# A feed-forward inside an attention stage changes its two PSUM banks and its place in every engine's order; a second one gets a second pair of activation buffers

## The reference

```
x += attention_a0(norm(x))   # 16 heads of 16, softmax
x += ffn0(norm(x))           # one 256x256 product with a bias
x += attention_b0(norm(x))   # 4 heads of 64, softmax, biases
x += ffn0(norm(x))           # the same weights again
x += retention_1(norm(x))    # 16 heads, decaying mask, no softmax
x += ffn1(norm(x))           # 256 -> 1024 gated, Hadamard, -> 256
x += attention_b1(norm(x))   # per token, over heads
x += ffn1(norm(x))
```

## Time and profile before

| | |
|---|---|
| median of 3 runs | 1296.91 us (1292.14 to 1298.73) |
| the profiled execution's own time | 1294.7 us |
| its span in the trace | 1292.9 us |
| PE busy | 1053.2 us, 81% |
| DVE busy | 696.3 us, 54% |
| ACT busy | 389.5 us, 30% |
| POOL busy | 321.3 us, 25% |
| mean granted clock of TensorE | 0.84 |

### The profile page before, as it was taken

One profiled execution on the slowest core, in us unless ns is written; L12 is line 12 of the kernel. 1 busy time (PEld: TensorE's weight loads), 2 busy tenths in 40 slices (PEclk: granted clock), 3 DMA queues, 4 the chain that ended last, 5 costly groups with the idle time before them and its releaser, 6 DMA issues.

```text
span 1292.9 us, 21462 instructions
## 1 busy us (share of the span) xinstructions
PE 1053.2 (81%) x8114; PEld 930.1 (72%) x8114; DVE 696.3 (54%) x1410; ACT 389.5 (30%) x711; POOL 321.3 (25%) x356
## 2 busy tenths in 40 slices
PE   3589878757887874688878999998888897789998
PEld 3466655456776764565656999997788887689998
DVE  4478765535455445587765554545455555534443
ACT  1146544412333220233324332322122221222332
POOL 5300100125633663312101021110033333332000
PEclk9679997859999996787777999986677775599999
DMA  8734320000010000174530000235656556210000
GB/s 237 223 117 145 118 86 3 1 1 17 18 66 17 1 1 0 58 209 135 142 113 1 1 1 1 56 76 98 122 112 120 109 111 118 37 33 10 17 18 17
DMA packets 147431, 89.39 MB, mean 69 GB/s; under 512 B 109632, under 2 KB 136256, under 8 KB 146560
## 3 DMA queue, kind: packets, MB, share of 16 engines
q1 hardware_dynamic: 142960, 70.45, 23.0%
q10 hardware_dynamic: 2944, 12.59, 3.4%
q0 software_dynamic: 1424, 4.98, 1.3%
HBM read 54.16 MB, written 33.55 MB: 68 GB/s over the span
## 4 chain that ended last, share of the span: by engine, by line
PE 63%; DVE 22%; issue 6%; ACT 4%; POOL 3%; DMA 1%; SPq 1%; ACTq 0%; DVEq 0%; POOLq 0%
PE SC L386 21%; PE SC L2055 9%; PE OT L386 7%; PE pb L386 5%; PE pa L386 3%; PE OT L1919 3%; DVE mx L1349 3%; PE SC L1903 2%; PE OT L2082 2%; PE SC L1874 2%; PE pa L2252 2%; DVE V L1515 1%; DVE r L1506 1%; PE OT L2351 1%; DVE Qs L1747 1%
## 5 line engine op out<-in xcount | busy, mean ns | idle before, releaser
L386 PE MATMUL SC<-xT_h,w_h 128*128 128x256 f32 x512 | 149.2, 291 | 8.1 <-DVE xT_l L1663 5.8
L386 PE MATMUL SC<-xT_l,w_h 128*128 128x256 f32 x512 | 147.2, 287 | 0.0
L386 PE MATMUL SC<-xT_h,w_l 128*128 128x256 f32 x512 | 146.5, 286 | 0.0
L386 PEld LDWEIGHTS SC<-xT_h,w_h 128*128 128x128 f32 x512 | 99.4, 194 | 11.5 <-DVE xT_l L1663 9.6
L386 PE MATMUL OT<-w,Qs 128*128 128x256 f32 x768 | 104.3, 285 | 2.2 <-DVE Qs L1673 1.4
L1349 DVE TENSOR_REDUCE mx<-SC 128x4 f32<-128x1024 f32 x64 | 78.1, 1221 | 45.9 <-PE SC L1874 45.9
L386 PEld LDWEIGHTS SC<-xT_h,w_l 128*128 128x128 f32 x512 | 99.6, 194 | 0.0
L386 PEld LDWEIGHTS SC<-xT_l,w_h 128*128 128x128 f32 x512 | 99.2, 194 | 0.0
L386 PEld LDWEIGHTS OT<-w,Qs 128*128 128x128 f32 x768 | 96.4, 191 | 2.9 <-DVE Qs L1673 1.6
L1669 DVE TENSOR_TENSOR hidden_f<-SC,silu_gate 128x512 f32<-128x512 f32 x64 | 44.0, 688 | 67.8 <-ACT silu_gate L1176 67.8
L774 POOL TENSOR_SCALAR ve<-mv 128x2 f32<-128x2 f32 x32 | 7.1, 222 | 294.7 <-DVE mv L1474 112.0
(11 more groups left out here) (406 smaller groups left out, 2882.4 us busy)
## 6 DMA issues: line engine op xcount, KB each, us to landing
Qs<-q_stack SPq DMA_DIRECT2D x56, 128.0 KB, 2.9
k_stack<-KT_h SPq DMA_DIRECT2D x16, 256.0 KB, 2.2
k_stack<-KT_l SPq DMA_DIRECT2D x16, 256.0 KB, 2.8
q_stack<-QT_h SPq DMA_DIRECT2D x16, 256.0 KB, 2.2
q_stack<-QT_l SPq DMA_DIRECT2D x16, 256.0 KB, 2.8
b_Q<-q_groups SPq DMA_DIRECT2D x64, 64.0 KB
o_groups<-b_O ACTq DMA_DIRECT2D x8, 512.0 KB, 3.0
Qs<-q_stack SPq DMA_DIRECT2D x56, 64.0 KB, 3.1
```

The source lines that it names most:

```text
L386: ins = pe.matmul(out_ap, left[a], right[b], start=first and n == 0, stop=last and n == len(terms) - 1, **more)
```

## The change

In F1 the turned rows go to OT1 (the bank of the maxima) and the product to pb (the bank of the values), no longer to pa and OT1. `x_turned` moves to slot 8b + 36, `x_high` and `x_low` to 8b + 37, `y_out` to 8b + 38. On TensorE F1's instructions now stand in front of those of A0S in a slot; on the other engines they stay behind. The waits are moved with the banks: A0S's `y_out` no longer waits for F1's `x_low`, `to_tokens` waits for F1's `x_low` of two sequences before in place of its residual, `a_turned` and `v_out` wait for F1's residual, F1's `x_turned` waits for divisions of A0S, its `y_out` for `al` and `ql`. VectorE makes A0S's divisions (`heads_out`) in front of the maximum of their slot. `prepared(2)` goes from slot 86 to 98. In F3 sequences take `aT` and `KT` in turn, `x_high(b)` waits for `y_out(b - 2)`, `y_out` and the residual come one slot later, the residual's wait is unchanged, and VectorE does `normalise` in front of `x_low`, the residual after both.

```diff
--- before.py
+++ after.py
@@ -446,17 +446,20 @@
             b, r = divmod(n + 32 - offset, 2)
             return [b] if r == 0 and 0 <= b < B else []
 
+        H_SLOTS = {F1: dict(stats=1, rstd=2, xn=3, bias=4, xT=5, low=6, y=7, res=7),
+                   F3: dict(stats=1, rstd=2, xn=3, bias=4, xT=4, low=5, y=7, res=8)}
+
         def h_psum(s, b):
 
-            return (pa[:], OT[1][:]) if s == F1 else (quarter[b % 2], quarter[2 + b % 2])
-
-        def h_pair(s):
-
-            return (W["r1_q"][0], W["r1_k"][0]) if s == F1 else aT
+            return (OT[1][:], pb[:]) if s == F1 else (quarter[b % 2], quarter[2 + b % 2])
+
+        def h_pair(s, b):
+
+            return (W["r1_q"][0], W["r1_k"][0]) if s == F1 else (aT, KT)[b % 2]
 
         def alone(eng, at, first, second):
 
-            for n in BAND:
+            for n in range(-24, 8 * B + 36):
                 at[first](n)
                 at[second](n)
 
@@ -872,9 +875,9 @@
                         .then_inc(sig.sem["h_xbias"], 1)
 
                 def at_slot(g):
-                    for b in due_between(s, g, 2):
+                    for b in due_between(s, g, H_SLOTS[s]["rstd"]):
                         rstd_of(b)
-                    for b in due_between(s, g, 4):
+                    for b in due_between(s, g, H_SLOTS[s]["bias"]):
                         row_bias(b)
                     if s == F1 and g == 84:
                         clear_wide()
@@ -1141,11 +1144,11 @@
 
                 def x_high(b):
                     wait("h_xT", b, 1)
-                    wait("h_y", b - 1, 1)
-                    act.activation(joined(h_pair(s)[0][:]), h_psum(s, b)[0], ACT.Copy).then_inc(sig.sem["h_xh"], 1)
+                    wait("h_y", b - (1 if s == F1 else 2), 1)
+                    act.activation(joined(h_pair(s, b)[0][:]), h_psum(s, b)[0], ACT.Copy).then_inc(sig.sem["h_xh"], 1)
 
                 def at_slot(g):
-                    for b in due_between(s, g, 5):
+                    for b in due_between(s, g, H_SLOTS[s]["low"]):
                         x_high(b)
                     if s == F1 and g == 70:
                         act.wait_ge(dve_setup, 2)
@@ -1438,6 +1441,10 @@
                     else:
                         for b in due(g, 9):
                             max_low(b)
+                        for b in due(g, 19):
+                            heads_out(b, 0)
+                        for b in due(g, 23):
+                            heads_out(b, 1)
                         for b, r in running(g, 0):
                             maximum(b, r)
                         for b in due(g, -16):
@@ -1446,10 +1453,6 @@
                             low(b, KT, pa, "kh", "kl")
                         for b in due(g, -11):
                             low(b, QT, pb, "qh", "ql")
-                        for b in due(g, 19):
-                            heads_out(b, 0)
-                        for b in due(g, 23):
-                            heads_out(b, 1)
                         for b in due(g, 26):
                             a_low(b)
                         for b in due(g, 30):
@@ -1576,8 +1579,8 @@
                     dve.tensor_copy(half_scale[64:128, :], lamt[64:128, 1:2]).then_inc(dve_setup, 1)
                 if part == 2:
                     dve.wait_ge(abs_ps, 1)
-                    dve.tensor_reduce(qscale[:, 0:1], pb[:, 0:3], AX.X, ALU.add).then_inc(abs_sum, 1)
-                    dve.tensor_copy(qscale[:, 1:2], pb[:, 3:4]).then_inc(abs_sum, 1)
+                    dve.tensor_reduce(qscale[:, 0:1], OT[1][:, 0:3], AX.X, ALU.add).then_inc(abs_sum, 1)
+                    dve.tensor_copy(qscale[:, 1:2], OT[1][:, 3:4]).then_inc(abs_sum, 1)
                     dve.wait_ge(abs_sum, 2)
                     dve.tensor_scalar(qscale[:, 0:1], qscale[:, 0:1], 1.0 / (3 * C * C), 1e-5, ALU.mult, ALU.max).then_inc(abs_sum, 1)
                     dve.tensor_scalar(qscale[:, 1:2], qscale[:, 1:2], 1.0 / (C * C), 1e-5, ALU.mult, ALU.max).then_inc(abs_sum, 1)
@@ -1608,7 +1611,7 @@
 
                 def x_low(b):
                     wait("h_xh", b, 1)
-                    pair = h_pair(s)
+                    pair = h_pair(s, b)
                     dve.tensor_tensor(joined(pair[1][:]), h_psum(s, b)[0], joined(pair[0][:]).bitcast(F32), ALU.subtract)\
                        .then_inc(sig.sem["h_xl"], 1)
 
@@ -1618,16 +1621,16 @@
                     dve.tensor_tensor(x[:, b, :], x[:, b, :], h_psum(s, b)[1], ALU.add).then_inc(sig.sem["h_xres"], 1)
 
                 def at_slot(g):
-                    for b in due_between(s, g, 5):
+                    for b in due_between(s, g, H_SLOTS[s]["xn"]):
+                        normalise(b)
+                    for b in due_between(s, g, H_SLOTS[s]["low"]):
                         x_low(b)
-                    for b in due_between(s, g, 7):
+                    for b in due_between(s, g, H_SLOTS[s]["res"]):
                         residual(b)
-                    for b in due_between(s, g, 3):
-                        normalise(b)
-                    for b in due_between(s, g, 1):
+                    for b in due_between(s, g, H_SLOTS[s]["stats"]):
                         stats(b)
-                    if s == F1 and g in (66, 72, 86):
-                        prepared((66, 72, 86).index(g))
+                    if s == F1 and g in (66, 72, 98):
+                        prepared((66, 72, 98).index(g))
                 return at_slot
 
             def ffn1(s):
@@ -1854,6 +1857,8 @@
 
                 def v_out(b):
                     wait("ql", b, 1)
+                    if s == A0S and b >= 6:
+                        item(pe, F1, "h_xres", b - 6, 1)
                     tokens_out(pb, xT, wv, "vp")
 
                 def loaded(b, r):
@@ -1926,7 +1931,7 @@
                     if half and not ret:
                         wait("normed", b, 1)
                         if b >= 2:
-                            item(pe, F1, "h_xres", b - 2, 1)
+                            item(pe, F1, "h_xl", b - 2, 1)
                     elif half:
                         if b == B - 1:
                             item(pe, F5, "g_xl", 0, 1)
@@ -1949,6 +1954,8 @@
                     wait("n2" if ret else "normed", b, 1 if ret else TT)
                     wait("vev", b + 4, 1)
                     wait("al", b - 1, 1)
+                    if s == A0S and b >= 2:
+                        item(pe, F1, "h_xres", b - 2, 1)
                     turn(ONr[b % len(ONr)], pb, "aT")
 
                 def y_out(b):
@@ -1959,8 +1966,6 @@
                         wait("normed", b + 2, 1)
                     else:
                         wait("kl", b + 5, 1)
-                        if b >= 1:
-                            item(pe, F1, "h_xl", b - 1, 1)
                     tokens_out(OT[1] if ret else pa, aT, wo, "y")
 
                 def at_slot(g):
@@ -2126,8 +2131,10 @@
                 def x_turned(b):
                     wait("h_xn", b, TT)
                     wait("h_xl", b - 1, 1)
-                    if s == F1 and b + 6 < B:
-                        item(pe, A0S, "kl", b + 6, 1)
+                    if s == F1:
+                        item(pe, A0S, "normed", min(b + 1, B - 1), TT)
+                        if b + 2 < B:
+                            item(pe, A0S, "normed", b + 2, 1)
                     turn(ON2, h_psum(s, b)[0], "h_xT")
 
                 def y_out(b):
@@ -2136,22 +2143,22 @@
                         if b == 0:
                             split_done(pe, "ffn0")
                         wait("h_xres", b - 1, 1)
-                        item(pe, A0S, "normed", min(b + 1, B - 1), TT)
-                        if b + 2 < B:
-                            item(pe, A0S, "normed", b + 2, 1)
+                        item(pe, A0S, "al", min(b + 1, B - 1), 1)
+                        if b + 6 < B:
+                            item(pe, A0S, "ql", b + 6, 1)
                     else:
                         wait("h_xres", b - 2, 1)
-                    tokens_out(h_psum(s, b)[1], h_pair(s), W["f0"], "h_y")
+                    tokens_out(h_psum(s, b)[1], h_pair(s, b), W["f0"], "h_y")
 
                 def at_slot(g):
-                    for b in due_between(s, g, 4):
+                    for b in due_between(s, g, H_SLOTS[s]["y"]):
+                        y_out(b)
+                    for b in due_between(s, g, H_SLOTS[s]["xT"]):
                         x_turned(b)
-                    for b in due_between(s, g, 6):
-                        y_out(b)
-                    if s == F1 and g == 85:
-                        whole(pe, A0S, "al")
+                    if s == F1 and g == 97:
+                        whole(pe, F1, "h_xl")
                         pe.wait_ge(abs_rows, 4)
-                        pe.matmul(pb[:, 0:4], ones[:], absum[:], start=True, stop=True).then_inc(abs_ps, 1)
+                        pe.matmul(OT[1][:, 0:4], ones[:], absum[:], start=True, stop=True).then_inc(abs_ps, 1)
```

(2 more changed lines are left out.)

## The result

The changed kernel took 1274.33 us (median of 4 runs, 1274.01 to 1276.96) against 1294.53 us for the kernel before on the same chip (4 runs, 1288.24 to 1298.73): a ratio of 0.9852, interval 0.9806 to 0.9899. The prediction said 1284, range 1277 to 1293.

A forecast was written before the change was run, and what follows sets the result against it. Hand-overs, not one full engine, were taken to bound the stretches changed. From a median of 1296.9 us, 12 for F3 and 0.4 beside A0S, 12.4 in all, gave 1284.5, said as 1284, range 1277 to 1293.

The forecast's parts named there:

- R1 costed at nothing: Behind F3: the chain into R1 moves forward with F3, and R1's rounds change by 0.
- The loop through GpSimd: F3: normalise, x_low, statistics, then GpSimd's rstd remain as the loop; a round takes 3.7 us, not 5.63, 13.5 us in all.
- the sign of being wrong: F3 rounds staying above 4.5 us, or stage 2 starting more than 4 us later, would show the prediction wrong.
- Beside A0S: the rounds: F1's first four sequences: -2.6 us for the first two together, 0 for the next two; division before maximum 3 costs 0.7.
- Beside A0S: the fifth sequence: F1's fifth turn waits for the division behind prepared(0); TensorE idles some 4 us, cost 4.3 us.
- Beside A0S: the end: Last A0S y_out loses its 1.50 us wait for x_low and the tail comes earlier: gain 2.1 us; prepared(2) costs 0.
- (a): R1's start gives back part of F3's gain, halving it: 1290.5 us, chance 0.15.
- (b): F3's second pair does nothing, a round stays near 5.6 us: 1296.5 us, chance 0.06.
- (c): F1's turn in front of the scores costs 2.7 us a period: slower, 1301, or 1311 with low clock; chance 0.06.
- (d): Denser F3 keeps TensorE at full clock, R1 starts 15 us earlier, joined stage gives 3: 1279 us, chance 0.13.
- the F3 term: F3: two buffer pairs and the new order gain 12 us, bounds 4 and 15.
- the joined term: Stage where F1 runs beside A0S: -0.4 us in all, bounds -4 and +4.

The follow-up runs named there:

- the repeated ones: Second profiles of the kernel before and of the changed kernel, no edit: 1294.3 us and 1274.5 us.
- the R1 edit: VectorE's heads_out(b, 1) put in front of R1's masked product: 1275.37 us on the kernel before, 1260.74 on the changed one, 1253.33 with bias and set-up moved too.
- after with heads_out first: Changed kernel with R1's heads_out(b, 1) in front of the masked product of its slot: 1260.74 us, ratio to before 0.9766.
- before again: The kernel before, unchanged, run and profiled a second time: 1294.3 us, ratio 1.0017.
- bias-first: Changed kernel with F3's bias add on GpSimd one slot earlier, in the slot of normalise: 1276.61 us, ratio to before 0.9877.
- the pair alone: Kernel before with only the second pair of activation buffers in F3, old slots and order: ratio to before 0.9926.
- set-up-later run: Changed kernel with prepared(0) moved from slot 66 to 71, its exponential from 70 to 73, prepared(1) from 72 to 75: ratio to before 0.9896.
- F3's part alone: Kernel before with only F3's edits (second pair, slots, VectorE's order), A0S and F1 as before: 1281.95 us, ratio to before 0.9928.

## Why the prediction was wrong, point by point

**What failed: R1 costed at nothing.** The step was "this tail is a chain behind F3's last x_low, on TensorE and VectorE, so it moves forward with F3", and everything behind it was taken as moved by the same amount. In the two profiles R1's rounds gave 10.1 of the 20.6 us by which the spans differ, and 9.4 of 23.2 in the repeated ones. Nearly half of the gain of these executions lies in a stage that the change doesn't touch.

What the runs showed in its place: the length of R1's rounds, with the same instructions, goes with TensorE's granted clock. In the fourteen profiles without the R1 edit it runs in step from 132.9 us at 0.87 to 143.0 at 0.76. As the clock has two levels, a mean of 0.76 over 143.0 us is some 69 us at the lower one, and 0.87 over 132.9 some 35. TensorE's idle time in the rounds isn't what shrank, it is 25.1 us before and 29.0 after; its busy time fell by 14.0. One sequence of R1 in the long rhythm takes 20.6 us at 0.75; before has three of the eight so, after has one, and after with heads_out first takes 16.4 to 16.6 us for the three.

The clock falls behind waits. Finer stretches of before, with columns as above, and the waits just ahead of its two falls, in the second stretch and in the fourth:

```profile
...
625.00:629.00 4.00, 2.95 (x36) 2.10 (x32) 3.84 (x11) 2.84 (x8) 0.72 (x2) 1.00 0.43 117
629.00:633.00 4.00, 3.54 (x26) 2.91 (x27) 3.02 (x10) 0.51 (x2) 1.47 (x4) 0.58 0.01 2
633.00:637.00 4.00, 2.39 (x20) 1.98 (x18) 1.42 (x4) 0.34 (x1) 0.39 (x1) 0.93 0.90 262
637.00:641.00 4.00, 4.00 (x32) 2.92 (x30) 3.69 (x9) 1.52 (x6) 1.00 (x2) 0.50 0.52 143
```
```profile
...
629.46 0.55 PE L1919 MATMUL OT<-pr,r_V 128*32 128x256 f32 x2 [0.69 <-DVE r_pr L1366]
...
635.40 0.36 PE L386 MATMUL pa<-xT_h,r_k_w 128*128 128x256 f32 x1 [1.61 <-DVE scratch L1376]
```

A wait of 1.61 us for heads_out, then a stretch at 0.50 (the lower level, 1.2 of 2.4 GHz), so the next products are slow. That VectorE then comes late again and the wait returns is my reading of it. The Trainium skill, page "TensorE: Matmul & The Clock Gate", section "HAM oscillation — how this bites in real kernels", describes such a cycle, with gaps that put TensorE back to half clock again and again; this stretch agrees, though here VectorE makes the gap and not a DMA. But the same wait doesn't always bring the fall. In after:

```profile
...
620.14 0.36 PE L386 MATMUL pa<-xT_h,r_k_w 128*128 128x256 f32 x1 [1.60 <-DVE scratch L1379]
```
```profile
...
621.00:638.00 17.00, 12.47 (x141) 9.44 (x141) 13.72 (x32) 7.33 (x21) 1.77 (x4) 1.00 0.53 165
```

The clock stays full for the 17 us behind it. All five waits for heads_out are there in both kernels, each as long to 0.01 us, in rounds that differ by 10.1. What the test shows is that most of the low clock goes with them: without 5.9 us of them the rounds are 19.8 us shorter in before and 11.5 in after, and TensorE's busy time gives 17.6 of the 19.8. The other runs fit: within a kernel the longer executions tend to have the lower mean clock (before again: 0.848 at 1288.1 us, 0.836 at 1303.1). No run sets the clock by itself, so that the clock is the cause and not a companion is the likeliest reading and not shown. It also stays open why after has the good rhythm in both its profiles and before in neither. Starting earlier isn't it by itself, as bias-first starts R1 earlier than after and has 141.1 in its profile.

**F3: the mechanism right, the size wrong.** I took 12 us, it was 7.3. The loop through GpSimd is the one named. The term that was mis-sized is `normalise`, 0.64 us predicted from its start to the next instruction's and 1.60 measured, which makes a full round 4.57 us and not 3.7. That is also just over the 4.5 us that I had named as the sign of being wrong. Over the seven gaps the residuals lie 30.2 / 7 = 4.31 us apart (the last ones are closer), so the rounds gave 39.4 - 30.2 = 9.2 us of my 13.5. Of these 1.9 were lost: 1.0 in front of the first residual, which comes a slot later, and 0.8 between the last one and R1. I had taken 1.5, and in another place. With the bias add moved, the residuals lie 3.44 us apart and the gain is 15.2, at my upper bound. I had read `normalise` at a place where it runs alone. The row that would have warned me is in the profile of before:

```profile
...
494.71 1.26 POOL L871 TENSOR_TENSOR x<-x,bf 128x512 f32<-128x512 f32 x1
495.05 1.39 DVE L1606 TENSOR_SCALAR ON<-x,g_mv,g_rstd 128x256 f32<-128x256 f32 x2
```

VectorE's two halves take 1.39 us beside GpSimd's add and 0.73 alone. The add here ends at 495.97 and `normalise` at 496.44, 0.47 later; in after the add ends at 497.14 and `normalise` at 497.62. So it is in all 56 places of the seventeen profiles where the two overlap in F3: `normalise` ends 0.47 to 0.48 us behind the add, whether it started 0.07 or 0.56 us after it, and takes 1.69 to 1.17 us accordingly. The Trainium skill, page "SBUF — State Buffer", section "🔬 SBUF: two separate sides", says that VectorE, in some of its instructions, and GpSimd share one pair of ports that one instruction holds to its end. The traces agree: the add keeps its 1.26 to 1.28 us, and it is `normalise` that is held until the add is through.

The claim "most of that loop comes from one pair of buffers and from VectorE's order" needs a correction as well. Either alone opens it. With the new order on top of the new pair the way to R1 is 2.5 us longer (52.6 against 50.1), though the rounds are 0.2 shorter each; that the bias add is to blame for it isn't shown, as no run has the pair alone with the add moved.

**Beside A0S: the rounds.** Predicted -2.6 for the first two sequences and 0 for the next two. First to fourth residual: 70.6 us before (143.0 to 213.6), 68.2 after: -2.4; in the repeated profiles 73.0 and 68.9, -4.1. But the working was not all right. Four of PE's waits in 132 to 217.7 us answer to the earlier trace rows:

```profile
...
PE pb L386 <- DVE r_k_w L1615: 3.7, 4, 1.0
PE OT L1888 <- DVE mx L1352: 3.7, 2, 1.8
PE SC L1879 <- DVE mx L1352: 3.3, 8, 1.0
PE OT L2259 <- DVE ON L1385: 1.8, 2, 1.5
```

to_tokens' wait for the residual is gone, as said, and y_out's wait for x_low has moved in front of the product into `pb` and is hardly longer (3.7 for 3.4). max_turned now waits for the maximum itself. And the division in front of maximum 3, which I costed at 0.7 us a period, earns its place: put back, the first three rounds take 72.0 us and not 68.2, and F1's turn waits 7.2 us in 4 times where it waited 1.8. My 0.7 a period had the wrong sign. I had taken the turn for hidden under the maximum whatever the division did. It isn't; it stands in front of the scores and needs the division first.

**Beside A0S: the fifth sequence.** Predicted: a gap of some 4 us in front of the fifth turn, cost 4.3. The timeline of all engines:

```profile
...
223.58 2.45 DVE L1569 TENSOR_REDUCE absum<-scratch 128x1 f32<-128x512 f32 x4
...
226.23 0.49 DVE L1385 TENSOR_TENSOR ON<-OT,rec 128x128 f32<-128x128 f32 x2
...
226.87 1.09 PE L2259 MATMUL OT<-ident,ON 128*128 128x128 f32 x4 [4.32 <-DVE ON L1385]
```

The gap is 4.32 us, behind the set-up's 2.45 us and the division, and fourth to fifth residual takes 25.1 us (210.5 to 235.6) where it took 21.5: +3.6. The set-up-later run removes it. This part was right.

**Beside A0S: the end.** Predicted -2.1, measured -4.4 (fifth to eighth residual 40.0 to 35.6 us; 38.9 to 35.6 in the repeated profiles). The order of these last periods gains more than the one wait that I counted; no run takes them apart. `prepared(2)`, which I costed at 0, now stands between the last residual and stage 2: its first statistics start 1.27 us behind that residual and not 0.79, a cost of 0.5. The whole stage came to -3.4 in place of -0.4, within its bounds. Over all profiles with before's joined stage, stage 2 starts at 272.3 to 278.3 (seven), mean 275.9; with the changed one, unrepaired (six), at 271.9 to 275.3, mean 273.0: -2.9. A single pair of profiles would have been weak evidence for this term: F3's part alone, with before's joined stage, starts stage 2 at 272.3.

**The rivals.** (a) gave half of F3's gain back at R1's start; R1's first scores start at 540.55 us, 10.7 earlier than before, which is the 3.4 and the 7.3. Of the 9.2 us that the rounds gave, 0.8 were lost there, not half. (b) and (c) fell: the turn in front of the scores costs neither its 2.7 us a period nor the clock. (d) was the nearest. It said "with a denser F3 TensorE stays at the full clock" and 3 us from the joined stage, 1279. The 3 us came. F3's clock stayed at 0.69; the clock rose one stage later, for a reason that (d) didn't have. So against the forecast the F3 term was 4.7 us too large, the joined term 3.0 too small, and 10 us of these profiles came from a stage costed at nothing.

## What to carry to other kernels

When a stretch becomes shorter, look at the next stage that is held by hand-overs before costing it at nothing: if the mean of its clock lies between the two levels, its length isn't fixed. Then try to remove a wait behind which the clock falls, which worked here in both kernels. Before one profile is taken for the kernel, compare its time and mean clock with those of the other runs. Before taking an instruction's time from one row, look for the same instruction beside GpSimd's work, and move the two apart. A wait in front of a long queue (the turn in front of the scores) makes its producer's place matter, even where the wait looks covered.

## What was not expected of the hardware

VectorE's `normalise` of 128 x 256 fp32, twice, took 0.73 us alone, 1.39 when GpSimd's add of 128 x 512 had started 0.34 us before it and 1.67 when it had started 0.07 before; it ended 0.47 us behind the add each time, and the add itself stayed at 1.26 to 1.28 us. The same 1036 records of TensorE were busy 117.9, 103.9, 100.2 and 96.5 us at clocks of 0.76, 0.87, 0.89 and 0.93. The same wait of TensorE, 1.60 us, was followed by the half clock in one place and by 17 us at the full clock in another. And one kernel's times can fall into two groups 9 us apart (F3's part alone), although each group is narrower than 4 us. The groups differ in mean clock too (0.853 to 0.858 and 0.845 to 0.849), which fits with R1 taking one of several rhythms from run to run; a profile of the second group that would show it wasn't taken.
